# Graph network on one core: the sums of 24 tiles scattered by SyncE, row by row, in place of GpSimd

## The reference

```python
w_m = (efeat @ W_msg + b_msg).reshape(E, in_f, -1)
w_a = (efeat @ W_attn + b_attn).reshape(E, in_f, -1)
h_src = feat[src][:, :, None]
e1, e2 = w_m * h_src, w_a * h_src
seg_max = jax.ops.segment_max(e2, dst, num_segments=N)
ex = jnp.exp(e2 - seg_max[dst])
denom = jax.ops.segment_sum(ex, dst, num_segments=N)
ft = jax.ops.segment_sum(e1 * (ex / denom[dst]), dst, num_segments=N)
...
x = _layernorm(x + ft.sum(axis=1))
x = _layernorm(x + segment_mean(edge_attr, dst))
```

## Time and profile before

| | us |
|---|---|
| median of 3 runs | 2244.83 (2243.46 to 2247.90) |
| the profiled execution, its own time | 2248.32 |
| its span, first to last instruction | 2246.4 |
| PE busy | 1962.2 (87%) |
| DVE busy | 1851.7 (82%) |
| ACT busy | 1256.2 (56%) |
| POOL busy | 1688.6 (75%) |
| DMA, mean rate | 21 GB/s |
| first of the 36 scatters into y_d | starts at 348.98 |
| last of them | starts at 1905.77 |

### The profile page before, as it was taken

The page is one execution under the profiler, slowest core; times in us unless marked ns, Lnnn a source line. Parts: engine busy times, 40 slices in busy tenths (PEclk is TensorE's granted clock), DMA queues, the critical chain, the costliest instruction groups (busy, mean ns, idle before and its releaser), DMA issues. The chain is left out here.

```text
span 2246.4 us, 21739 instructions
## 1 busy us (share of the span) xinstructions
PE 1962.2 (87%) x6682; PEld 900.0 (40%) x6682; DVE 1851.7 (82%) x2907; ACT 1256.2 (56%) x1228; POOL 1688.6 (75%) x1845
## 2 busy tenths in 40 slices
PE   1667989898999899999989998999989898989995
PEld 0423434343444444444444443444434343444442
DVE  7767788687788888899888888888878787999985
ACT  4444555455565556656656654556555555556653
POOL 6777777777777777777777777777777777777776
PEclk9778999999999999999999999999999999999998
DMA  6200000000000100001001000001000010101000
GB/s 232 87 13 13 13 16 13 13 13 13 13 13 13 19 12 13 12 13 18 12 12 17 12 12 13 15 12 16 12 12 16 12 15 13 35 11 22 14 7 4
DMA packets 60072, 47.59 MB, mean 21 GB/s; under 512 B 28366, under 2 KB 55439, under 8 KB 59436
## 3 DMA queue, kind: packets, MB, share of 16 engines
q0 software_dynamic: 57632, 29.73, 8.7%
q1 hardware_dynamic: 2316, 16.38, 2.0%
HBM read 44.00 MB, written 1.90 MB: 20 GB/s over the span
## 5 line engine op out<-in xcount | busy, mean ns | idle before, releaser
L661 POOL DMA_INDIRECT AR<-in_xt,AR x1607 | 1539.9, 958 | 493.2 <-issue 448.3
L1135 PE MATMUL PX<-AR,CS 128*128 128x512 f32 x3246 | 1552.4, 605 | 6.5 <-ACT AR L901 6.3
L1479 DVE CUSTOM_DVE_ANT_1 AR<-PW,AR 128x1024 f32<-128x1024 f32 x815 | 975.1, 1220 | 162.3 <-PE PW L1115 111.6
L1135 PEld LDWEIGHTS PX<-AR,CS 128*128 128x128 f32 x3246 | 623.6, 193 | 567.9 <-issue 444.5
L1115 PE MATMUL PW<-WS,LT 100*128 100x512 bf16 x1630 | 507.8, 397 | 197.3 <-DVE AR L1479 196.1
L1492 DVE TENSOR_TENSOR AR<-AR,PX 128x1024 f32<-128x1024 f32 (+1 forms) x442 | 501.3, 1134 | 78.8 <-ACT PX L951 54.2
L895 ACT ACTIVATE LT<-PTB 100x1024 bf16<-100x1024 bf16 (+1 forms) x221 | 211.2, 956 | 502.6 <-PE PTB L1104 502.6
L953 ACT ACTIVATE AR<-AR 128x2048 f32<-128x2048 f32 (+1 forms) x221 | 413.0, 1869 | 7.2
L957 ACT ACTIVATE PX<-AR 128x1024 f32<-128x1024 f32 (+1 forms) x221 | 212.4, 961 | 327.3 <-DVE AR L1492 324.5
L1115 PEld LDWEIGHTS PW<-WS,LT 100*128 100x128 bf16 x1630 | 144.6, 100 | 570.1 <-issue 288.0
L951 ACT ACTIVATE PX<-AR 128x1024 f32<-128x1024 f32 (+1 forms) x221 | 231.1, 1046 | 21.5 <-DVE AR L1492 19.4
(11 more groups left out here) (192 smaller groups left out, 508.4 us busy)
## 6 DMA issues: line engine op xcount, KB each, us to landing
AR<-in_xt,AR POOLq DMA_INDIRECT x1607, 2.3
AR<-in_eat SPq DMA_DIRECT2D x3, 3128.0 KB, 12.7
AR<-in_eat SPq DMA_DIRECT2D x1, 3120.0 KB
y_d<-AR SPq DMA_DIRECT2D x1, 784.0 KB, 14.1
AR<-y_d SPq DMA_DIRECT2D x1, 784.0 KB, 4.6
AR<-in_es,E0I POOLq DMA_INDIRECT x48, 3.5
y_d<-AR POOLq DMA_INDIRECT x36, 2.1
CS<-in_cst SPq DMA_DIRECT2D x1, 442.0 KB, 5.0
```

Of the source, the lines that this page charges most:

```text
L661: g.indirect_dma_start(feat(h, j - j0, j - j0 + 1), None, xt, bass.IndirectOffsetOnAxis(ap=node, axis=0)).then_inc(hg_sem(h), 16)
L1135: i = pe.matmul(PDR, IDN, x, start=(a == 0 and j == 0), stop=(g == LAST[k] and j == n - 1))
L1479: v.tensor_tensor_reduce(em(g, j, j + 2).rearrange("p (x c) -> p x c", c=32), w, hb, 1.0, LOW, ALU.mult, ALU.max, accum_out=MXC[:, k % 2, ...
```

## The change

POOL's `results` are left out for the first 24 tiles (BYROW). SP does their scatters: in three batches of eight tiles, when the results of all eight are there, it goes through the 128 partitions, loads the eight node numbers of a partition from NODE into registers, and issues for each one a transfer of 32 words from OUTR to the row of YD at that number. Before it loads XNN and YN, it waits for all these transfers (d_row), and for POOL's 12 remaining scatters.

```diff
+BYROW = 24
...
+        d_row = d_bl[0:3]
...
             def regular():
-                sp.wait_ge(S["d_y"], 16 * MAIN)
+                nodes = [sp.alloc_register(f"node_{x}") for x in range(8)]
+                sp.wait_ge(S["d_yz"], 16)
+                for b in range(BYROW // 8):
+                    sp.wait_ge(S["a_out"], 8 * b + 8)
+                    sp.wait_ge(S["v_sa"], 8 * b + 8)
+                    for p in range(128):
+                        sp.reg_load(nodes, NODE[p:p + 1, 8 * b:8 * b + 8])
+                        for x in range(8):
+                            at = sp.snap(nodes[x], min_val=0, max_val=NP - 1)
+                            sp.dma_start(YD[bass.DynSlice(at, 1), :], OUTR[p:p + 1, 8 * b + x, :]).then_inc(d_row[b], 16)
+                for b in range(BYROW // 8):
+                    sp.wait_ge(d_row[b], 16 * 128 * 8)
+                sp.wait_ge(S["d_y"], 16 * (MAIN - BYROW))
                 sp.dma_start(XNN, xt[0:NP, :].rearrange("(p c) k -> p c k", c=NC)).then_inc(S["d_xn"], 16)
...
                 for k in range(1, NC):
                     feats(k)
-                    if 5 <= k < MAIN + 5:
+                    if BYROW + 5 <= k < MAIN + 5:
                         results(k - 5)
```

## The result

The changed kernel takes 3041.95 us (median of 4, 3041.58 to 3043.68), the kernel before 2246.36 on the same chip: 1.355 times as long, interval 1.353 to 1.357. The forecast was 2848, its range 2350 to 3500. (Of the 18 runs of the kernel before that stand beside experiments 1 to 4, one took 8804 us; it is in no ratio.)

What follows compares the result with a forecast made beforehand. POOL's queue was taken as the bound from some 1265 us; SP's 3072 rows at 0.615 us would delay DVE's main norm step by 603.4 us: 2246.4 + 603.4 = 2849.8 span, 2848 us as median, range 2350 to 3500.

Steps and rivals of the forecast that it cites:

- The bound of before: POOL's queue of gathers and scatters is the bound from some 1265 us on; each slot removed ahead is worth 1.30 us.
- The limit of 0.41 us a row: On SP, 3072 rows must go in 1255 us, before DVE's main norm step at about 1904: 0.41 us a row.
- The place and the kind of the stall: At DVE's first main norm step: one new wait of about 600 us for YN, PE, DVE and POOL idle 1900 to 2540.
- The work behind it: After DVE's first step of the main norm, the same 311.0 us of work remains, kept whole.
- The price of a row: On SP, one row costs 0.615 us, between 0.315 and 0.875, so the last row is issued at 2531.7.
- transfer and address: On SP, per row: 0.455 us for the transfer, as for the last three stores, and 0.05 for the address instruction.
- share of the load of eight words: On SP, one load of eight node numbers takes 0.9 us, spread over eight rows: 0.11 us a row.
- a far end: On SP, each loaded word costs 0.9 us by itself, a row 0.8 more; end at 5275 us.
- Rival A: SP keeps up, a row under 0.41 us; POOL's 31.2 us are won whole, 2214 us; chance 0.11.
- Rival B: A row costs far more: load paid by the word (5275 us), or rows landing slowly (3724 at 0.9 us); chance 0.10.
- The floor of about 600 ns: For SP's register loads, the skill's floor would give 0.075 us a row, not 0.11, and some 110 us less.

Runs made afterwards that it cites:

- experiments 1 to 4: Against the changed kernel: 8 tiles on SP, 2233.12 us; 16 tiles, 2346.8; rows without their loads, 2267.37; 8 tiles' rows to an unread tensor, POOL scattering all 36, 2243.17.
- experiment 6: Against the changed kernel: SP's rows and its waits for them left out too, so nobody does the 24 scatters; 2213.59 us, ratio 0.9868 to the kernel before.
- experiment 3: Against the changed kernel: registers loaded once a batch instead of 384 loads, rows sent to counted-up addresses in another DRAM tensor; 2267.37 us.
- experiment 1: Against the changed kernel: BYROW 8 instead of 24, so SP scatters one batch of eight tiles; 2233.12 us, ratio 0.996 to the kernel before.

## Why the prediction was right, and where it was off

**The bound of before.** "So from some 1265 us on POOL's queue is the bound": shown by experiment 6. DVE's waits for gathers fell from 99.5 us in all to 71.2 there, 28.3 of the 29.4 us won:

```profile
DVE AR L1479 <- DMA AR<-in_xt,AR: 71.2, 13, 16.2
```

**The limit of 0.41 us a row.** Right for 24 tiles. Each experiment has its own limit by the same sum, and they stand on both sides of it: with 16 tiles in batches of eight it is (2040.3 - 127.8 - 7.1 - 643.5) / 2048 = 0.616, the row at 0.679 is over it by 0.063, and 2048 of them make 129 us where the wait was 127.8; with batches of four it is (1912.2 - 7.1 - 406.6) / 2048 = 0.732, and the row at 0.731 just keeps it; with 8 tiles the rows were out 560 us before POOL's last scatter. DVE came to its step at 1900.9 where the forecast had 1904, and the rows were to be out 7.1 us ahead of it. From the last row at 2726.1 to DVE at 2733.2 it is 7.1, by luck, since two errors cancel: the rows had landed 1.2 us after the last issue and not 2.1, and YN took 5.3 and not 4.6.

**The place and the kind of the stall.** Right: one wait, at L1566; DVE, PE and ACT idle; POOL stopping once its ring was full (its next gather, at 2735.7, had waited 772.6 us for DVE). In the hole POOL still issues 49 instructions (columns: stretch and length in us, then busy of PE, PEld, DVE, ACT, POOL, clock, DMA share, GB/s):

```profile
1902.00:2732.00 830.00, 0.00 (x0) 0.00 (x0) 0.00 (x0) 0.00 (x0) 46.24 (x49) 0.50 0.01 3
2733.00:3040.00 307.00, 266.70 (x868) 121.35 (x868) 266.95 (x434) 169.58 (x178) 181.81 (x268) 0.95 0.06 9
```

**The work behind it.** 311.0 forecast, 306.7 measured. The forecast kept it whole and allowed the lead of POOL "at most a few us"; it was worth about those 4. Behind the step DVE waited 3.3 us for gathers before and not at all after the hole, and in experiment 6, with the same 24 slots won and no hole, 311.9 us lie behind the step. In the three runs with a hole it is 304.3 to 306.7, in the five without one 307.9 to 311.9. So it is probably the lead that POOL got in the hole, and not the slots, that shortened it; no run tests this by itself.

**The price of a row: the term that was mis-sized.** Forecast 0.455 + 0.05 + 0.11 = 0.615, measured 0.679, and the parts are off by more than the sum, in opposite directions; that the sum came out within 0.07 is in part luck:

| part | forecast | measured |
|---|---|---|
| transfer and address | 0.505 | 0.427 (experiment 3) |
| share of the load of eight words | 0.11 | 0.25 |
| a row | 0.615 | 0.679 |

The load was the term that was mis-sized: "For eight words I take all 0.9". One word takes 0.27 to 0.47 us, four 1.15, eight 1.98. From four to eight that is 0.21 a word, on top of some 0.3; this would make 0.53 of one word, which took less. In the forecast a load by the word stood only as a far end, at 0.9 a word, and the true price lay between. The row that bounds it from above, 0.9 us at the branch, holds for one word and says nothing of a second. The transfer went the other way: I took the nearest three stores, of 0.43 us each, and the issues of the rows are half as dear, 0.224 us of SP each.

The sum over all terms: the last row 2726.1 - 2531.7 = 194.4 us later than forecast, the work behind 4.3 shorter, together 190.1 = 3039.9 - 2849.8.

**Rival A** (SP keeps up) did not come for 24 tiles, but it is what happens for 8 and, in batches of four, for 16. Its worth was forecast at 31.2 us and measured at 29.4. The Trainium skill ("DMA: Bandwidth & Descriptors", "Issuing engines are not separate DMA queues") calls the sequencer's time to initiate a DMA usually small relative to the DMA itself. The 1024 starts of experiment 1 cost nothing, as by that rule; the 3072 of the change, 2086 us in one queue, set the end, so whether the time is small is also a question of how many starts stand for one. **Rival B** put the load at a price by the word, or had the rows land more slowly than SP issues them. The first came true in kind and not in size: 0.21 us a word, not 0.9. The second fell: SP waited 0.8 us for its last rows.

The floor of about 600 ns that the Trainium skill ("DMA: Bandwidth & Descriptors", "Latency and other measured facts") gives a tensor_load was weighed in the forecast. No run here shows such a floor: one word took 0.27 us in experiment 3 and 0.47 at the branch.

## What to carry to other kernels

An idle sequencer is not a free one: count what one instruction of the full engine becomes there (here 1.30 us of POOL became 128 rows at 0.68 us, 87 us of SP), add it up from the moment its input is ready, and put it against the moment its result is asked for. Up to that point the work is free and the slots won are worth their full length; beyond it every further row is paid in full by all engines, because the wait stands in the queue of DVE, which all of them need. So size such a move by the deadline, start it as early as the first inputs allow, and price loads of registers by the word.

## What the runs showed of the hardware

- A load of registers from SBUF on SP: 0.27 to 0.47 us for one word, 1.15 for four, 1.98 for eight. The one at the branch:

```profile
L434 SPq TENSOR_LOAD <-TOT x1: 472/472/472, 81.7 to 81.7; - x1
```

- A transfer of one row of 128 bytes with a register address holds SP for 0.224 us when such issues follow each other, 0.427 from one to the next with its address instructions (53 and 29 ns in experiment 3) and all gaps, where SBUF to SBUF issues took 0.675. The first row of all took 0.33 (at 640.55), the first behind the next load 0.27.
- PE's clock: in the hole it is granted at 0.50, the lower of its two levels (1.2 GHz of 2.4). PE takes up work at 2735.5 after 833.8 us of standing still, and its first two pairs of products take 1.03 and 1.06 us; the third, at 2743.29, takes 0.60 again, as before the hole; the granted clock is 0.74 from 2733 to 2750 and 0.97 from 2750 to 2800:

```profile
2735.47 1.03 PE L1129 MATMUL PW<-WS,LT 100*128 100x512 bf16 x2 [833.80 <-DVE AR L1493]
...
2739.70 1.06 PE L1129 MATMUL PW<-WS,LT 100*128 100x512 bf16 x2
...
2743.29 0.60 PE L1129 MATMUL PW<-WS,LT 100*128 100x512 bf16 x2
```
```profile
2733.00:2750.00 17.00, 14.54 (x43) 6.70 (x44) 13.83 (x22) 7.26 (x9) 9.49 (x10) 0.74 0.05 5
2750.00:2800.00 50.00, 43.04 (x147) 19.74 (x145) 48.24 (x81) 29.09 (x32) 33.89 (x35) 0.97 0.07 11
```

What stays open: why the issue of a row is cheaper than that of a store of 0.43 us (the rows are smaller, have a register address and follow each other, and no run parts these), and how many rows a microsecond the gathers would bear; neither was tried.
